# The opening microseconds of a decayed linear-attention layer: smaller idle matmuls that may start sooner, and three small steps moved on VectorE and ScalarE

## The chip, the cores and the metric

One NeuronCore of a Trainium2 chip runs the whole kernel. The metric is the device time of one execution in microseconds, from three runs of the same compiled program; their median is the time before. Five engines work side by side, each in its own program order: TensorE (PE in the rows, its weight loads PEld), VectorE (DVE), ScalarE (ACT), GpSimd (POOL) and SyncE (SP), which issues the transfers. They meet only at semaphores.

## The reference

A layer on x of shape 4 x 512 x 256 (batch, tokens, width), 16 heads of 16 columns. Cut to what matters:

```
xn = layernorm(x)
q, k, v = silu(xn @ Wq), silu(xn @ Wk), silu(xn @ Wv)
# per head, chunks of tokens, log_decay ld (one number per head):
#   scores = (q k^T) * exp(ld * max(i - j, 0)) * (i >= j)      inside a chunk
#   o      = scores v + (q S) * exp(ld * (i + 1))              S: state of the chunks before
#   S      = exp(ld * chunk) * S + (k * exp(ld * (chunk - 1 - i)))^T v
o = rmsnorm_per_head(o * sigmoid(xn @ Wg1 @ Wg2)) * norm_w
s = o @ Wo
g = silu(fp8(xn * scale) @ fp8(W2 * scale1) / (scale * scale1))
out = x + s * g
```

## The kernel before, in words

**Stages.** The work is cut into 8 steps: two pairs of sequences, four blocks of 128 tokens each; a step `n` holds one block of both sequences of a pair (256 tokens). Inside a step two chunks of 64 tokens are worked on side by side. Each engine has one program written out by hand, with steps overlapped: while step `n` is scored and read out, step `n+1` is projected and step `n+2` is normalised and transposed. The order on an engine is the order of the code; nothing else schedules it. This case is about the first 15 us, before step 0 reaches its first scores, and about one place near 25 us.

**Precision.** Weights and activations are split into a high part and a rest (`w_hi`, `w_lo`; `xT_hi`, `xT_lo`), and a product is three matmuls: high by high, high by low, low by high. The high part of Wq and Wv is made on VectorE, that of Wk on ScalarE (`high_w(1)`); all three rests on VectorE (`low_w`).

**The opening, engine by engine.**

- GpSimd makes constants; a counter `s_pool` rises by one with most of them. `minus_half`, `minus_one` and `eps_col` (128x2 each) are done at 4, the 128x128 identity `ident` at 6.
- TensorE waits for 6, runs `idle(43, ...)`, 43 fp32 matmuls of the first 32 columns of `ident` on themselves, whose result is never read; then `transpose_x(0)`, which needs both normalised tiles `xn` (one from ScalarE, one from VectorE); then `keep_warm(2, ...)`, again unread; then `project_q(0)`, 12 matmuls, once `xT_hi` and `w_lo` of Wq are there; then 12 for k transposed, once `w_lo` of Wk is there; then 12 for k in natural order, then `scores(0)`. Each fp32 matmul shows as two in the trace, so 43 show as 86.
- VectorE makes statistics, log decays per position, its tile of `xn`, the split of Wq, `lag_logdecay` (128x1024: lag times log decay for all heads), `xT_lo` of step 0, the rest of Wk, statistics of step 1, `decay_mask` (128x1024, from ScalarE's `lag_decay`), the split of Wv, the copies of Wg1 (`wg1_a`, `wg1_b`), then `exponent(0)` and `magic(0)` (fp8 rounding, from `e4_y`), then the four `mask(0, r)`, which turn scores into `probs`.
- ScalarE makes its tile of `xn`, small exponentials, `xT_hi` of step 0, `w_hi` of Wk, `lag_decay = exp(lag_logdecay)`, loads the table of Silu, and then `q_par` (twice), `kT`, `e4_y`, `k_nat`.
- GpSimd, after the factors for step 1, takes `sum_y(0)`, `round_y(0)`, `decay_k(0)`, `decay_q(0)` and so on, starting with the result of `magic(0)`.

`inv_scales` and `descale` (128x2 and 128x1, from the two scalar inputs) are needed by `silu_ffn(1)` on ScalarE near 27 us; VectorE makes them just ahead of `w2_fp8`, the last step of rounding W2, for which GpSimd's `own_state_end(0)` waits too. In the rows, `e4_` is cut to `e_`, `w2_` and `w_f32` to `w_` and `w_f`, `wg1_` to `wg_`.

Of the kernel before, what the change touches and what calls it, by code (L numbers as in the profile page):

```python
# [9 lines left out]
ALU = mybir.AluOpType  # L10
# [7 lines left out]
def layer_kernel(nc, x, log_decay, Wq, Wk, Wv, Wo, Wg1, Wg2, norm_w, W2, scale, scale1, out):  # L18
# [29 lines left out]
    with ExitStack() as ctx:  # L48
        def sb(name, shape, dt=F32):
            return ctx.enter_context(nc.sbuf_tensor(name, shape, dt))  # L50

        def sem(name):
            return ctx.enter_context(nc.semaphore(name))
# [3 lines left out]
        w_f32 = sb("w_f32", [P, 3, KH, D])  # L57
        w_hi = sb("w_hi", [P, 3, KH, D], F32R)
# [28 lines left out]
        scales = sb("scales", [P, 2])  # L87
        inv_scales = sb("inv_scales", [P, 2])
        descale = sb("descale", [P, 1])
        ld_row = sb("ld_row", [P, H])  # L90
        ld_col = sb("ld_col", [P, KH])
        ident = sb("ident", [P, P])
# [11 lines left out]
        pos_col = sb("pos_col", [P, 1])  # L104
        pos_col64 = sb("pos_col64", [P, 1])
        k_logdecay = sb("k_logdecay", [P, H])
# [8 lines left out]
        minus_half = sb("minus_half", [P, 2])  # L115
# [57 lines left out]
        ps_score = [b_s[:, 0:512], b_s[:, 512:1024], b_o[:, 0:512], b_o[:, 512:1024]]  # L173
# [32 lines left out]
        s_w = [sem(f"w{name}_loaded") for name in "qkv"]  # L206
# [5 lines left out]
        s_scale = [sem(f"scale{n}_loaded") for n in range(2)]  # L212
        s_pool = sem("pool_constants")
        s_dvec = sem("dve_constants")
# [5 lines left out]
        s_whi = [sem(f"w{name}_hi_ready") for name in "qkv"]  # L220
# [84 lines left out]
        def need(eng, s, v):  # L305
            if v > 0:
                eng.wait_ge(s, v)
# [10 lines left out]
        def x_tiles(n):  # L318
            first = S * NB * pair(n) + pos(n)
            return slice(first, first + NB + 1, NB)  # L320
# [245 lines left out]
        def _(act):  # L566
# [11 lines left out]
            def high_xT(n):  # L578
                act.wait_ge(s_xTps, n + 1)
                need(act, s_vps, n - 1)  # L580
                a.activation(xT_hi[:, n % 2], ps_xT, ACT.Copy).then_inc(s_xThi, 1)
# [99 lines left out]
            def high_w(n):  # L681
                act.wait_ge(s_w[n], 16)
                a.activation(w_hi[:, n], w_f32[:, n], ACT.Copy).then_inc(s_whi[n], 1)
# [12 lines left out]
            a.activation(chunk_decay[:], ld_col[:], ACT.Exp, scale=float(C)).then_inc(s_actc, 1)  # L696
            a.activation(k_decay[:], k_logdecay[:], ACT.Exp).then_inc(s_actc, 1)
            high_xT(0)
            high_w(1)
            act.wait_ge(s_laglog, 1)  # L700
            a.activation(lag_decay[:], lag_logdecay[:], ACT.Exp).then_inc(s_actc, 1)
            a.activation(table_load[:, 1:2], eps_col[:, 0:1], ACT.Silu)
            act.wait_ge(s_qps, 1)
            act.wait_ge(s_hpar, 2)
# [81 lines left out]
        def _(dve):  # L786
            v = nc.vector
# [15 lines left out]
            def low_xT(n):  # L803
                dve.wait_ge(s_xThi, n + 1)
                need(dve, s_vps, n - 1)
                v.tensor_tensor(xT_lo[:, n % 2], ps_xT, xT_hi[:, n % 2].bitcast(F32), ALU.subtract).then_inc(s_xTlo, 1)  # L806

            def exponent(n):
                dve.wait_ge(s_y4, n + 1)
                v.tensor_scalar(e4_exp[:].bitcast(I32), e4_y[:, n % 2].bitcast(I32), 0x7F800000, None, ALU.bitwise_and).then_inc(s_exp, 1)  # L810

            def magic(n):
                dve.wait_ge(s_exp, n + 1)
                need(dve, s_e4q, n - 1)
                v.tensor_scalar(e4_magic[:, n % 2], e4_exp[:], E4_MIN, E4_MAGIC, ALU.max, ALU.mult).then_inc(s_e4, 1)  # L815
# [8 lines left out]
            def low_g1(n):  # L824
                dve.wait_ge(s_g1hi, n + 1)
                v.tensor_tensor(g1T[32:64], ps_g1T[32:64], g1T[32:64].bitcast(F32), ALU.subtract).then_inc(s_g1lo, 1)
# [166 lines left out]
            def low_w(n):  # L993
                dve.wait_ge(s_whi[n], 1)
                v.tensor_tensor(w_lo[:, n], w_f32[:, n], w_hi[:, n].bitcast(F32), ALU.subtract).then_inc(s_wlo, 1)
# [23 lines left out]
            for half in range(KH):  # L1019
# [1 line left out]
            dve.wait_ge(s_ldown, KH)  # L1021
            v.tensor_reduce(ld_col[:], ld_own[:], AX_X, ALU.add)
            dve.wait_ge(s_pool, 11)
            v.tensor_scalar(k_logdecay[:], ld_row[:], pos_col[:, 0:1], None, ALU.mult).then_inc(s_dvec, 1)
            v.tensor_copy(ld_units[:].rearrange("p (r k q) -> p r k q", r=4, k=2),
                          ld_row[:].rearrange("p (k r q) -> p r k q", k=2, r=4))
            dve.wait_ge(s_shift, 1)
            v.tensor_scalar(xn[:, 0, 1], x_sb[:, x_tiles(0).start + NB, :], rstd[:, 0, 1:2], shift[:, 0, 1:2], ALU.mult, ALU.add).then_inc(s_xnfirst, 1)
            dve.wait_ge(s_w[0], 16)
            v.tensor_copy(w_hi[:, 0], w_f32[:, 0]).then_inc(s_whi[0], 1)  # L1030
            low_w(0)

            dve.wait_ge(s_dvec, 2)
            v.tensor_tensor(lag_logdecay[:], lag_clamped[:].unsqueeze(1).broadcast_to([P, H, C]),
                            ld_units[:].unsqueeze(2).broadcast_to([P, H, C]), ALU.mult).then_inc(s_laglog, 1)
            low_xT(0)
            low_w(1)
            stats(1)
# [13 lines left out]
                              wg1_f32[:].unsqueeze(2).broadcast_to([P, KH, 3, GR])).then_inc(s_g1w, 1)  # L1052
            dve.wait_ge(s_g1w, 1)
            v.tensor_tensor(wg1_a[:, :, 96:96 + GR], wg1_f32[:], wg1_a[:, :, 0:GR].bitcast(F32), ALU.subtract).then_inc(s_g1w, 1)
            exponent(0)
            magic(0)

# [23 lines left out]
            dve.wait_ge(s_w2sum, 1)  # L1081
            v.scalar_tensor_tensor(out=w2_q[:], in0=w2_f32[:], scalar=-1.0, in1=w2_m[:], op0=ALU.mult, op1=ALU.add).then_inc(s_w2q, 1)
            low_g1(1)
            v.reciprocal(inv_scales[:], scales[:]).then_inc(s_dvec, 1)
            dve.wait_ge(s_dvec, 3)
            v.tensor_scalar(descale[:], inv_scales[:, 0:1], inv_scales[:, 1:2], None, ALU.mult).then_inc(s_dvec, 1)
            dve.wait_ge(s_w2q, 5)
            v.scalar_tensor_tensor(out=w2_fp8[:], in0=w2_over[:], scalar=0.0, in1=w2_q[:], op0=ALU.mult, op1=ALU.add).then_inc(s_w2q, 1)
            put_nan(1)
# [35 lines left out]
            n = STEPS - 1  # L1125
# [20 lines left out]
        def _(pe):  # L1146
            t = nc.tensor

            def transpose_x(n):
                pe.wait_ge(s_xn, n + 1)  # L1150
                if n == 0:
                    pe.wait_ge(s_xnfirst, 1)
                if n == 1:
                    pe.wait_ge(s_y4, 1)
                need(pe, s_on, n - 2)
                if n == 2:
                    pe.wait_ge(s_y4, 2)
                for s in range(S):
                    for kk in range(KH):
                        mm = t.transpose(ps_xT[:, kk, s * P:s * P + P], xn[:, n % 2, s, kk * P:kk * P + P], ident[:])  # L1160
                mm.then_inc(s_xTps, 1)
# [265 lines left out]
            def idle(count, dst):  # L1427

                for _ in range(count):
                    t.matmul(dst[0:32, 0:32], ident[:, 0:32], ident[:, 0:32], start=True, stop=True)  # L1430

            def keep_warm(count, dst):
                for _ in range(count):
                    t.matmul(dst[:, 0:P], ident[:], ident[:], start=True, stop=True)

            pe.wait_ge(s_pool, 6)
            idle(43, ps_score[1])
            transpose_x(0)
            keep_warm(2, ps_score[1])
            pe.wait_ge(s_wlo, 1)  # L1440
# [3 lines left out]
            for part in (w_hi, w_lo):  # L1444
                for half in range(KH):
                    for kk in range(KH):
                        t.matmul(ps_kT[:, half], part[:, 1, kk, half * P:half * P + P], xT_hi[:, 0, kk],
                                 start=(part is w_hi and half == 0 and kk == 0), stop=False, skip_group_check=True)
            for half in range(KH):
                for kk in range(KH):  # L1450
                    mm = t.matmul(ps_kT[:, half], w_hi[:, 1, kk, half * P:half * P + P], xT_lo[:, 0, kk],
                                  start=False, stop=(kk == KH - 1), skip_group_check=True)
# [68 lines left out]
            n = STEPS - 1  # L1521
# [48 lines left out]
```

## Time and profile before

| | us |
|---|---|
| median of 3 runs | 124.86 |
| lowest, highest | 124.48, 125.65 |
| the profiled execution, its whole time | 124.32 |
| its span, first to last instruction | 122.6 |

Busy time in that span: TensorE 114.2 us, VectorE 97.6, GpSimd 89.9, ScalarE 85.0. The profiled execution is 0.54 us below the median of the three, and 1.72 us of its time lie outside the span. A busy share is a mean over the whole span; the change touches the first 15 us, so what counts there is which engine has no idle time in that stretch and which wait ends last.

### The profile page before, as it was taken

The page shows a single profiled execution, that of the slowest core. Times are in us where ns is not written, and L with a number is a line of the kernel's source. Part 1 is how long each engine was busy: PE and PEld are TensorE (multiplying, and loading weights), DVE is VectorE, ACT ScalarE, POOL GpSimd, SP SyncE. Part 2 cuts the span into 40 slices and gives each one's busy share as a digit, 9 for nine tenths or more (in the row PEclk, how much of TensorE's full clock was granted, in tenths as well). Part 3 has the DMA queues.
Part 4 walks back from the last instruction along what each step waited for, and adds up shares of the span by engine and source line. Part 5 has one row for each costly group of instructions (what it writes and reads, how often), then busy time and mean ns, then how long its engine had stood idle before and what let it go on. Part 6 is the DMA issues. An engine that isn't in the chain of part 4 may idle for free.

```text
span 122.6 us, 6549 instructions
## 1 busy us (share of the span) xinstructions
PE 114.2 (93%) x2756; PEld 100.6 (82%) x2756; DVE 97.6 (80%) x264; ACT 85.0 (69%) x164; POOL 89.9 (73%) x126
## 2 busy tenths in 40 slices
PE   3989989998999999999999999999999999899890
PEld 3989879876998899879988898879988997787670
DVE  1899899999998698949994989679975985388572
ACT  7679989889996758766886667685776377932200
POOL 6615499979999899688969696969882996544140
PEclk9999999999999999999999999999999999999999
DMA  2669910002000220024001500042003405000214
GB/s 86 201 176 324 327 38 3 0 5 51 3 5 0 50 46 0 5 56 126 0 3 31 145 5 5 5 92 87 0 5 68 114 0 135 1 5 5 88 34 142
DMA packets 11085, 7.59 MB, mean 62 GB/s; under 512 B 4848, under 2 KB 11056, under 8 KB 11056
## 3 DMA queue, kind: packets, MB, share of 16 engines
q1 hardware_dynamic: 11056, 7.17, 21.1%
q8 instruction: 22, 0.36, 1.3%
q14 instruction: 7, 0.06, 0.2%
HBM read 3.50 MB, written 2.10 MB: 46 GB/s over the span
## 4 chain that ended last, share of the span: by engine, by line
POOL 33%; issue 27%; PE 16%; DVE 15%; ACT 6%; POOLq 0%; DVEq 0%
POOL qd L440 5%; POOL e_sum L430 5%; POOL y L468 5%; POOL kd L446 4%; PE b_s L1430 4%; DVE probs L831 3%; POOL own_mid L450 3%; POOL probs L473 2%; POOL rstd L417 2%; PE b_s L1423 2%; PE b_o L1423 2%; PE b_s L1272 1%; POOL own_end L450 1%; PE b_kv L1342 1%; DVE og L864 1%
## 5 line engine op out<-in xcount | busy, mean ns | idle before, releaser
L1187 PE MATMUL b_kv<-w_hi,xT_hi 128*128 128x256 f32 x64 | 16.6, 283 | 0.0
L1188 PE MATMUL b_kv<-w_lo,xT_hi 128*128 128x256 f32 x64 | 16.4, 280 | 0.0
L430 POOL TENSOR_TENSOR e_sum<-e_y,e_magic 128x512 f32<-128x512 f32 x8 | 10.3, 1286 | 7.4 <-DVE e_magic L815 7.2
L864 DVE SCALAR_TENSOR_TENSOR og<-gate_tanh,b_o 128x512 f32<-128x512 f32 x7 | 4.8, 687 | 11.0 <-PE b_o L1342 11.0
L1190 PE MATMUL b_kv<-w_hi,xT_lo 128*128 128x256 f32 x64 | 12.7, 280 | 0.0
L1342 PE MATMUL b_o<-probs,v_par 64*32 64x64 f32 x896 | 12.4, 223 | 0.0
L1187 PEld LDWEIGHTS b_kv<-w_hi,xT_hi 128*128 128x128 f32 x64 | 12.1, 189 | 0.2 <-issue 0.2
L1188 PEld LDWEIGHTS b_kv<-w_lo,xT_hi 128*128 128x128 f32 x64 | 12.1, 190 | 0.0
L468 POOL TENSOR_TENSOR y<-sg,x_sb 128x512 f32<-128x512 f32 x7 | 9.0, 1288 | 3.9 <-DVE sg L991 3.9
L479 POOL TENSOR_TENSOR on_lo<-on,on_hi 128x512 fp32r<-128x512 f32 x6 | 7.7, 1278 | 5.1 <-ACT on_hi L679 5.1
L435 POOL TENSOR_TENSOR e_q<-e_sum,e_magic 128x512 bf16<-128x512 f32 x8 | 10.8, 1348 | 0.5
L831 DVE TENSOR_TENSOR probs<-b_o,decay_mask 128x512 f32<-128x512 f32 x16 | 10.3, 685 | 1.0 <-PE b_o L1272 0.9
L1342 PEld LDWEIGHTS b_o<-probs,v_par 64*32 64x32 f32 x896 | 9.0, 105 | 2.3 <-issue 1.2
L440 POOL TENSOR_TENSOR qd<-q_silu,q_decay 128x512 f32<-128x512 f32 x8 | 10.4, 1305 | 0.0
L1272 PE MATMUL b_s<-q_par,kT 32*64 32x128 f32 x256 | 9.3, 276 | 1.1 <-DVE og L864 0.7
L596 ACT ACTIVATE q_par<-b_q,head_parity 128x512 f32<-128x512 f32 x16 | 10.1, 683 | 0.0
L473 POOL TENSOR_TENSOR probs<-scores_copy,decay_mask 128x512 f32<-128x512 f32 x7 | 9.1, 1300 | 0.9 <-ACT scores_copy L645 0.9
L1190 PEld LDWEIGHTS b_kv<-w_hi,xT_lo 128*128 128x128 f32 x64 | 9.7, 188 | 0.0
L1272 PEld LDWEIGHTS b_s<-q_par,kT 32*64 32x64 f32 x256 | 7.6, 130 | 2.5 <-issue 2.2
L1272 PE MATMUL b_o<-q_par,kT 32*64 32x128 f32 x256 | 9.6, 278 | 0.0
L586 ACT ACTIVATE e_y<-b_x,scales 128x512 f32<-128x512 f32 x8 | 5.5, 688 | 5.3 <-DVE xT_lo L806 5.3
L591 ACT ACTIVATE q_silu<-b_q 128x512 f32<-128x512 f32 x8 | 4.8, 599 | 6.3 <-PE b_q L1179 6.3
(218 smaller groups left out, 378.7 us busy)
## 6 DMA issues: line engine op xcount, KB each, us to landing
out_dram<-y SPq DMA_DIRECT2D x7, 256.0 KB, 2.4
x_sb<-in_L_attn_x_dram SPq DMA_DIRECT2D x4, 384.0 KB, 6.1
own_cross<-own_end SPq DMA_DIRECT2D x12, 64.0 KB, 2.2
qd_cross<-qd SPq DMA_DIRECT2D x12, 64.0 KB, 2.2
x_sb<-in_L_attn_x_dram SPq DMA_DIRECT2D x2, 128.0 KB, 2.1
w_f<-in_L_attn_Wq_dram SPq DMA_DIRECT2D x1, 256.0 KB, 3.6
w_f<-in_L_attn_Wk_dram SPq DMA_DIRECT2D x1, 256.0 KB, 3.8
x_sb<-in_L_attn_x_dram SPq DMA_DIRECT2D x1, 256.0 KB, 4.0
```

The source lines that it names most:

```text
L430: g.tensor_tensor(e4_sum[:], e4_y[:, n % 2], e4_magic[:, n % 2], ALU.add).then_inc(s_e4sum, 1)
L435: g.tensor_tensor(e4_q[:], e4_sum[:], e4_magic[:, n % 2], ALU.subtract).then_inc(s_e4q, 1)
L440: g.tensor_tensor(qd[:, n % 2].rearrange("p k (s t) -> p k s t", s=S), q_silu[:].rearrange("p k (s t) -> p k s t", s=S), q_decay[:].unsque ...
L468: g.tensor_tensor(y[:, n % 2], sg[:, n % 2].rearrange("p (s d) -> p s d", s=S), x_sb[:, x_tiles(n), :], ALU.add).then_inc(s_y, 1)
L473: g.tensor_tensor(probs[:, 1], scores_copy[:].rearrange("p (s z) -> p s z", s=S), decay_mask[:, 1].unsqueeze(1).broadcast_to([P, S, 4 * C] ...
L596: a.activation(q_par[:, n % 2, par], ps_q, ACT.Silu, scale=head_parity[:, par:par + 1]).then_inc(s_qpar, 1)
L831: v.tensor_tensor(probs[:, r], ps_score[r].rearrange("p (s z) -> p s z", s=S), decay_mask[:, r].unsqueeze(1).broadcast_to([P, S, 4 * C]), ...
L1187: t.matmul(dst[:, s], xT_hi[:, u, kk, tok], w_hi[:, w, kk], start=(s == 0 and kk == 0), stop=False, skip_group_check=True)
L1188: t.matmul(dst[:, s], xT_hi[:, u, kk, tok], w_lo[:, w, kk], start=False, stop=False, skip_group_check=True)
L1190: mm = t.matmul(dst[:, s], xT_lo[:, u, kk, tok], w_hi[:, w, kk], start=False, stop=(kk == KH - 1), skip_group_check=True)
L1272: mm = t.matmul(ps_score[r][c * C:c * C + C, cols], kT[rows, u, half, tok], q_par[rows, u, :, half, tok], start=True, stop=True, skip_grou ...
L1342: mm = t.matmul(dst[32 * r:32 * r + 32, c, z:z + C], v_par[rows, u, blk:blk + 2 * E], probs[rows, r, s, i:i + C], start=(half == 0 and s = ...
```

## The change

Three edits. (1) The idle matmuls take the 128x2 tile `minus_half` as both operands instead of 128x32 of `ident`, and wait for `s_pool` 4 instead of 6; there are still 43 of them. The wait for 6 stays, now behind them. (2) On VectorE `ld_units` goes ahead of `k_logdecay`, and `lag_logdecay` ahead of the split of Wq; on ScalarE `lag_decay` goes ahead of `high_w(1)`. (3) On VectorE the reciprocals and `descale` go from behind `low_g1(1)` to ahead of `exponent(0)`, with a wait for the two loads of the scales.

```
@@ ScalarE
             high_xT(0)
-            high_w(1)
             act.wait_ge(s_laglog, 1)
             a.activation(lag_decay[:], lag_logdecay[:], ACT.Exp).then_inc(s_actc, 1)
+            high_w(1)
@@ VectorE
-            v.tensor_scalar(k_logdecay[:], ld_row[:], pos_col[:, 0:1], None, ALU.mult).then_inc(s_dvec, 1)
             v.tensor_copy(ld_units[:].rearrange("p (r k q) -> p r k q", r=4, k=2),
                           ld_row[:].rearrange("p (k r q) -> p r k q", k=2, r=4))
+            v.tensor_scalar(k_logdecay[:], ld_row[:], pos_col[:, 0:1], None, ALU.mult).then_inc(s_dvec, 1)
             dve.wait_ge(s_shift, 1)
...
+            dve.wait_ge(s_dvec, 2)
+            v.tensor_tensor(lag_logdecay[:], lag_clamped[:].unsqueeze(1).broadcast_to([P, H, C]),
+                            ld_units[:].unsqueeze(2).broadcast_to([P, H, C]), ALU.mult).then_inc(s_laglog, 1)
             dve.wait_ge(s_w[0], 16)
             v.tensor_copy(w_hi[:, 0], w_f32[:, 0]).then_inc(s_whi[0], 1)
             low_w(0)
-            dve.wait_ge(s_dvec, 2)
-            v.tensor_tensor(lag_logdecay[:], ...
             low_xT(0)
...
+            for n in range(2):
+                dve.wait_ge(s_scale[n], 16)
+            v.reciprocal(inv_scales[:], scales[:]).then_inc(s_dvec, 1)
+            dve.wait_ge(s_dvec, 3)
+            v.tensor_scalar(descale[:], inv_scales[:, 0:1], inv_scales[:, 1:2], None, ALU.mult).then_inc(s_dvec, 1)
             exponent(0)
             magic(0)
...
             low_g1(1)
-            v.reciprocal(inv_scales[:], scales[:]).then_inc(s_dvec, 1)
-            dve.wait_ge(s_dvec, 3)
-            v.tensor_scalar(descale[:], inv_scales[:, 0:1], inv_scales[:, 1:2], None, ALU.mult).then_inc(s_dvec, 1)
@@ TensorE
-                    t.matmul(dst[0:32, 0:32], ident[:, 0:32], ident[:, 0:32], start=True, stop=True)
+                    t.matmul(dst[0:2, 0:2], minus_half[:], minus_half[:], start=True, stop=True)
...
+            pe.wait_ge(s_pool, 4)
+            idle(43, ps_score[1])
             pe.wait_ge(s_pool, 6)
-            idle(43, ps_score[1])
             transpose_x(0)
```

What stands in a row on VectorE at the opening (`ld_row` is the row of log decays, `w_f` the loaded weights, Wq first and Wk at the second `w_lo`), and behind the copies of Wg1:

```order
-L1024 TENSOR_SCALAR k_logdecay<-ld_row,pos_col 128x16 [waits pool_constants]
-L1025 COPY ld_units<-ld_row 128x16
+L1024 COPY ld_units<-ld_row 128x16 [waits pool_constants]
+L1026 TENSOR_SCALAR k_logdecay<-ld_row,pos_col 128x16
 L1028 TENSOR_SCALAR xn<-x_sb,rstd,shift 128x256 [waits rstd_shift_ready]
-L1030 CAST w_hi<-w_f 128x512 [waits wq_loaded]
+L1031 TENSOR_TENSOR lag_logdecay<-lag_clamped,ld_units 128x1024 [waits dve_constants]
+L1034 CAST w_hi<-w_f 128x512 [waits wq_loaded]
 L995 TENSOR_TENSOR w_lo<-w_f,w_hi 128x512 [waits wq_hi_ready]
-L1034 TENSOR_TENSOR lag_logdecay<-lag_clamped,ld_units 128x1024 [waits dve_constants]
 L806 TENSOR_TENSOR xT_lo<-b_x,xT_hi 128x512 [waits xT_hi_ready]
```

The 128x1024 product has moved ahead of both steps of Wq's split; behind `xT_lo` nothing has moved until this piece, still on VectorE:

```order
 L1051 CAST wg_b<-wg_f 128x2x3x16
 L1054 TENSOR_TENSOR wg_a<-wg_f,wg_a 128x2x16 [waits wg1_stack_ready]
+L1057 RECIPROCAL inv_scales<-scales 128x2 [waits scale1_loaded,scale0_loaded]
+L1059 TENSOR_SCALAR descale<-inv_scales 128x1 [waits dve_constants]
 L810 TENSOR_SCALAR e_exp<-e_y 128x512 [waits e4_y_ready]
 L815 TENSOR_SCALAR e_magic<-e_exp 128x512 [waits e4_exp_ready]
```

Two steps now stand ahead of `exponent(0)`. On ScalarE, between the small exponentials and the load of Silu's table:

```order
 L697 ACTIVATE k_decay<-k_logdecay 128x16
 L581 ACTIVATE xT_hi<-b_x 128x512
+L700 ACTIVATE lag_decay<-lag_logdecay 128x1024
 L683 ACTIVATE w_hi<-w_f 128x512
-L701 ACTIVATE lag_decay<-lag_logdecay 128x1024
 L702 ACT_TABLE_LOAD
 L702 ACTIVATE table_load<-eps_col 128x1
```

The exponential of the lags and the high part of Wk have changed places; all around them is as it was.

## Rows read from the trace of the kernel before

**Rows 1.** The chain that ended last, opening: start us, us, what

```profile
2.12 4.79 PE b_s L1430 x86
...
7.66 0.60 ACT xT_hi L581
...
8.67 1.05 ACT lag_decay L701
...
9.74 1.28 ACT L702
...
12.88 0.58 ACT e_y L586
```

**Rows 2.** Busy time by engine (PE, PEld, DVE, ACT, POOL), granted clock, in two stretches

```profile
5.00:8.30 3.30, 3.07 (x44) 2.81 (x42) 3.12 (x10) 2.03 (x7) 0.52 (x7) 1.00 0.82 252
8.30:13.00 4.70, 4.54 (x44) 4.37 (x46) 4.67 (x12) 4.67 (x8) 2.84 (x6) 1.00 0.87 263
```

**Rows 3.** VectorE in order of time, opening: start us, us, what

```profile
5.61 0.41 DVE L1028 TENSOR_SCALAR xn<-x_sb,rstd,shift 128x256 f32<-128x256 f32 x1
5.94 0.42 DVE L1030 CAST w_hi<-w_f 128x512 fp32r<-128x512 f32 x1
6.39 0.69 DVE L995 TENSOR_TENSOR w_lo<-w_f,w_hi 128x512 fp32r<-128x512 f32 x1
7.00 1.22 DVE L1034 TENSOR_TENSOR lag_logdecay<-lag_clamped,ld_units 128x1024 f32<-128x1024 f32 x1
8.29 0.69 DVE L806 TENSOR_TENSOR xT_lo<-b_x,xT_hi 128x512 fp32r<-128x512 f32 x1
8.89 0.68 DVE L995 TENSOR_TENSOR w_lo<-w_f,w_hi 128x512 fp32r<-128x512 f32 x1
...
12.83 0.18 DVE L1054 TENSOR_TENSOR wg_a<-wg_f,wg_a 128x32 fp32r<-128x32 f32 x1
13.49 0.43 DVE L810 TENSOR_SCALAR e_exp<-e_y 128x512 int32<-128x512 int32 x1 [0.48 <-ACT e_y L586]
...
14.30 1.28 DVE L831 TENSOR_TENSOR probs<-b_o,decay_mask 128x512 f32<-128x512 f32 x2
```

**Rows 4.** GpSimd in order of time: a constant, and the start of rounding

```profile
1.39 0.09 POOL L487 MEMSET eps_col<- 128x2 f32 x1
...
14.46 1.30 POOL L430 TENSOR_TENSOR e_sum<-e_y,e_magic 128x512 f32<-128x512 f32 x1 [1.50 <-DVE e_magic L815]
```

**Rows 5.** TensorE in order of time, opening

```profile
6.84 0.78 PE L1160 MATMUL b_x<-ident,xn 128*128 128x128 f32 x4
7.46 0.61 PE L1434 MATMUL b_s<-ident 128*128 128x128 f32 x4
8.40 0.71 PE L1174 MATMUL b_q<-xT_hi,w_hi 128*128 128x256 f32 x4 [0.33 <-ACT xT_hi L581]
...
9.89 0.63 PE L1447 MATMUL b_kv<-xT_hi,w_hi 128*128 128x256 f32 x4
...
13.86 0.28 PE L1272 MATMUL b_o<-q_par,kT 32*64 32x128 f32 x2
...
15.54 0.60 PE L1160 MATMUL b_x<-ident,xn 128*128 128x128 f32 x4
```

**Rows 6.** ScalarE in order of time, opening

```profile
5.41 0.60 ACT L691 ACTIVATE xn<-x_sb,shift,rstd 128x256 f32<-128x256 f32 x1 [1.17 <-POOL shift L419]
...
6.59 0.20 ACT L697 ACTIVATE k_decay<-k_logdecay 128x16 f32<-128x16 f32 x1
...
8.15 0.62 ACT L683 ACTIVATE w_hi<-w_f 128x512 fp32r<-128x512 f32 x1
```

**Rows 7.** VectorE in order of time, near 25 us

```profile
24.62 0.17 DVE L1084 RECIPROCAL inv_scales<-scales 128x2 f32<-128x2 f32 x1
...
24.95 0.88 DVE L1088 SCALAR_TENSOR_TENSOR w_fp<-w_over,w_q 128x512 bf16<-128x512 bf16 x1
```

**Rows 8.** GpSimd in order of time, near 25 us

```profile
25.91 0.61 POOL L450 TENSOR_TENSOR own_end<-state_end,own_quad 128x256 f32<-128x256 f32 x1 [0.63 <-DVE w_fp L1088]
```

**Rows 9.** The chain that ended last, near 25 us

```profile
25.31 0.61 ACT b_s L603
```

More of the change, by code:

```diff
@@ L1031, in _ @@
             low_w(0)
-            dve.wait_ge(s_dvec, 2)
-            v.tensor_tensor(lag_logdecay[:], lag_clamped[:].unsqueeze(1).broadcast_to([P, H, C]),
-                            ld_units[:].unsqueeze(2).broadcast_to([P, H, C]), ALU.mult).then_inc(s_laglog, 1)
             low_xT(0)
```

## The prediction

> **What bounds the kernel now.** I read three views, in this order. First the chain that ended last, because it names what a reader would cut: in the opening it runs through the idle matmuls (86 rows, 4.79 us), `xT_hi` on ScalarE, `lag_decay`, the table load and `e_y` [rows 1]. Read alone, it promises that shorter idle matmuls and an earlier `lag_decay` pass straight on to the end. The second view is the busy time by stretch [rows 2], which shows what the chain can't: a second engine with no slack. VectorE is busy 3.12 of 3.30 us in the first stretch and 4.67 of 4.70 in the second, while ScalarE is busy 2.03 of 3.30 in the first. The third is VectorE in order of time [rows 3]: from `xn` at 5.61 to the last copy of Wg1, which ends at 12.83 + 0.18 = 13.01, its steps stand shoulder to shoulder; its only real pause is the 0.48 us ahead of `e_exp` at 13.49, where it waits for ScalarE's `e_y`. GpSimd starts its long row of 1.3 us products at 14.46, on the result that follows this `e_exp` [rows 4]. So the time at which `e_exp` starts stands for the end of the opening: before 13.49, VectorE needs 13.01 and ScalarE 13.46. A change that frees ScalarE alone can win at most 0.48 us there, less what it adds to VectorE.
>
> **Idle matmuls.** Now they start when `ident` is done, at 2.12, and end at 6.91. The new ones need only `eps_col`, done at 1.39 + 0.09 = 1.48 [rows 4], so they start 0.6 us sooner. What one with two columns takes no row shows. Upper bound: what one of 32 columns takes, 4.79 / 86 = 56 ns; they then end at 1.5 + 4.8 = 6.3. Lower: four with 128 columns take 0.61 us, 153 ns each [rows 5]; a straight line through 32 and 128 columns falls by 1 ns a column and gives 25 ns for two, 2.2 us in all, an end near 3.7. I take no value between, since for the next step both ends are near the same: the transposes need both tiles of `xn`, which end at 5.41 + 0.60 = 6.01 on ScalarE [rows 6] and at 5.61 + 0.41 = 6.02 on VectorE [rows 3]. They start at 6.05 (6.3 at the upper bound) in place of 6.84, a gain of 0.8 (0.55). The wait for `s_pool` 6 behind the idle matmuls costs nothing: `ident` is long done.
>
> **Lags ahead of weights, ScalarE.** `xT_hi` started 7.66 - 6.84 = 0.82 behind the first transpose [rows 1, 5]; now at 6.87, and ScalarE is free from 6.59 + 0.20 = 6.79 [rows 6]. `lag_decay` follows 0.49 later, as `w_hi` did (8.15 - 7.66), at 7.36; its input is there, since `lag_logdecay` now runs from 5.94 and takes 1.22 [rows 3], to 7.16. `high_w(1)` starts 1.07 behind it (9.74 - 8.67), at 8.43, and ends at 9.05. The table load follows 0.52 behind its start, at 8.95 in place of 9.74. So ScalarE's lead is 0.79 us, and `e_y` ends at 12.88 + 0.58 - 0.79 = 12.67.
>
> **Lags ahead of weights, VectorE.** The order changes, not the sum: 5.94 + 1.22 (lags) + 0.45 (`w_hi`) + 0.61 (`w_lo`) = 8.22, where `lag_logdecay` ended before, too (7.00 + 1.22). `xT_lo` waited for `xT_hi` until 8.29 and no longer does: 0.07 gained. `w_lo` of Wq moves from 7.08 to about 8.30, and `project_q(0)` waits for that now and not for `xT_hi`: it starts at 8.3, before 8.40 [rows 5]. So TensorE gets back 0.1 of the 0.8. Then comes the price. The rest of Wk waits for its high part, which ScalarE now has at 9.05 and had at 8.15 + 0.62 = 8.77: that step starts at 9.08, before 8.89. VectorE stands there for 0.2 us, with the statistics of step 1, `decay_mask` and the split of Wv queued behind it: +0.19 on all of them, and the copy of Wg1 ends at 13.20. If the transposes start at 6.3, 0.25 later, it is +0.44. TensorE's matmuls for k transposed start with that `w_lo`, at 9.8, before 9.89. GpSimd clears `wg1_a` and `wg1_b` when `lag_logdecay` is done, sooner now, in a stretch where it has 0.52 us of work in 3.30 [rows 2]: nothing.
>
> **Reciprocals sooner.** Two steps, from 24.62 to 24.95 [rows 7]: 0.33 us, now ahead of `e_exp`. Their new wait for the scales costs nothing, since ScalarE uses the first for `e_y` itself, and the second is issued with the loads of the first 8 us; if it came late, `e_exp` and the masks would stand behind it. Sum for `e_exp`: 13.20 + 0.33 = 13.53, against 13.49 before. **The pause of 0.48 us is used up**, 0.19 by the later Wk and 0.33 by the reciprocals. At the bounds: 13.01 - 0.07 + 0.33 = 13.27 (-0.22) with no stall on Wk, and 13.01 + 0.44 + 0.33 = 13.78 (+0.29) with the late transposes. The masks then start at 14.34, before 14.30; the scores ended at 13.86 + 0.28 = 14.14 [rows 5], and come a little sooner.
>
> Near 25 us 0.33 is given back, but `w_fp` also waits for ScalarE's `w_over`, so I count 0.13 of it. GpSimd's `own_end` waited for `w_fp` until 25.91 [rows 8] and moves up by that. The chain doesn't pass there: it goes through ScalarE's `b_s` at 25.31 [rows 9], which neither gives way to `w_fp` nor follows it. 0 at the end; bounds 0 and -0.13.
>
> **Sum.** +0.04 at the opening, 0 near 25 us; bounds -0.35 and +0.29. Every later step follows by the same waits, so this is also the sum for the end. I take the middle of the bounds, -0.03: the profiled execution, 124.32 (span 122.6), becomes 124.3; the median of the runs, 0.54 above it, 124.86 becomes **124.8**.
>
> **Rivals.** (a) *ScalarE's lead arrives.* If VectorE's row is elastic (steps that run faster when GpSimd is quiet, or a stall on Wk that doesn't come), the chain of waits is right and up to 0.79 us goes to the end: 124.86 - 0.8 = 124.1. For it: [rows 1]. Against it: [rows 2, 3], and 0.33 us of new work at the very place.
>
> (b) *The small matmul isn't shorter.* If one with two columns takes 56 ns as now, the change doesn't shorten the idle stretch, only shifts it by 0.6: `e_exp` at 13.78, 124.86 + 0.3 = 125.1. For it: the rows of 128 and 32 columns say nothing of a floor. Against it: the straight line.
>
> (c) *TensorE's clock, the slower side.* The rows grant 1.00, the 2.4 GHz level, in both stretches [rows 2], with TensorE at work without a pause from 2.1 to 8.1. The four first transposes took 0.78 us, the four at 15.54 took 0.60 [rows 5], so I don't take for certain that the first ones ran at the full pace. After the change TensorE works on two columns at a time and may then stand from about 3.7 to 6.05, 2.3 us that were filled before. If the level is 1.2 GHz when the projections come, their 36 matmuls, which take 9.89 - 8.40 = 1.49 us per 12, take up to twice that. With half of the 36 at the low level: 2.2 us more; the scores have 14.30 - 14.14 = 0.16 of slack and start 0.3 sooner, so 1.7 reaches the masks: 126.6. It passes 1% (1.25 us) from about 14 matmuls at the low level on; all 36 give 129. The page "TensorE: Matmul & The Clock Gate" of the Trainium skill speaks for this rival (section "What's actually happening"): "the default state is throttled, and activity releases the throttle." No row here shows a fall or a rise, so I can't say from the trace whether such small matmuls hold the clock; that they are the kernel's only work in those microseconds is what makes this the widest risk.
>
> **Chances.** Forecast 0.48, (a) 0.17, (b) 0.15, (c) 0.20. A measurement of this kernel tells about 1% from no change; the three runs before spread by 0.9%. Forecast, (b) and most of (a) lie within 1%. Faster by over 1%: 0.06 from (a), where other luck adds to it, and 0.02 from the forecast, 0.08. Slower: 0.17 from (c), 0.02 from (b), 0.19. Within: 0.73. Range: from (a) less 0.5 for the spread of the runs, 123.6, up to 126.2, which takes in (b) and the cheap part of (c).
>
> **What would show it.** In the profile after: idle matmuls from 1.5, transposes at 6.05 to 6.3; `lag_decay` near 7.4; the second `w_lo` waiting for ScalarE until 9.1; the table load near 9.0; `e_exp` between 13.3 and 13.8 with no wait for `e_y` ahead of it; `e_sum` at 14.5. (a) is right if `e_sum` starts before 14.1, (b) if the idle matmuls still take 4.8, (c) if the projections' starts lie further apart than 0.12 us or the granted clock is below 1.00. Wrong altogether would be a gain over 1.2 us: then a loop later than 15 us would have fallen into another rhythm, which no term here covers.

## Result, and the profile after

| | before | after |
|---|---|---|
| median of the runs taken together, us | 124.72 (6 runs, 124.44 to 125.65) | 126.30 (6 runs, 125.87 to 126.90) |
| ratio, 95% interval | | 1.0126, 1.0081 to 1.0171 |
| profiled execution, us | 124.32 | 126.31 |
| its span, us | 122.6 | 124.5 |

The change makes the kernel slower by 1.6 us at the medians. The time was forecast as 124.8, with 123.6 to 126.2 as the range; the outcome is the rival (c), TensorE's clock. Here and in the experiments a ratio leaves out the runs more than 1.5% above the fastest of the same kernel, while the medians are of all runs.

TensorE in order of time in the changed kernel, opening (the columns are start us, us, what):

```profile
1.54 2.29 PE L1432 MATMUL b_s<-minus_half 128*2 128x2 f32 x86 [1.54 <-POOL eps_col L487]
6.31 1.08 PE L1162 MATMUL b_x<-ident,xn 128*128 128x128 f32 x4 [2.49 <-DVE xn L1028]
7.19 1.06 PE L1436 MATMUL b_s<-ident 128*128 128x128 f32 x4
8.42 1.22 PE L1176 MATMUL b_q<-xT_hi,w_hi 128*128 128x256 f32 x4 [0.17 <-DVE w_lo L995]
9.44 1.05 PE L1176 MATMUL b_q<-xT_hi,w_lo 128*128 128x256 f32 x4
10.29 1.05 PE L1181 MATMUL b_q<-xT_lo,w_hi 128*128 128x256 f32 x4
11.15 1.05 PE L1450 MATMUL b_kv<-xT_hi,w_hi 128*128 128x256 f32 x4
12.00 0.90 PE L1450 MATMUL b_kv<-xT_hi,w_lo 128*128 128x256 f32 x4
12.74 0.63 PE L1454 MATMUL b_kv<-xT_lo,w_hi 128*128 128x256 f32 x4
```

The idle matmuls end at 3.8 and TensorE stands for 2.49 us. Then read the starts, not the busy time: four 256-column matmuls take 11.15 - 10.29 = 0.86 us from start to the next group's start, 0.215 each, which is 256 columns at 1.2 GHz; before, [rows 5], the first row of such matmuls and the row of the k projection are 12 matmuls and 1.49 us apart, 0.12 each, 256 columns at 2.4 GHz. From 12.00 to 12.74 four take 0.74, so the pace changes inside them, near 12.6: three at 0.215, one at 0.12. By then 19 of the 36 matmuls of the projections have been started at the lower level. The first transposes, too, take 0.88 from start to start of the next group, where those of [rows 5] took 7.46 - 6.84 = 0.62 and those of a later step less still.

The granted clock of the windows of the changed kernel (the 1.00 ahead of the last two numbers) says nothing of it:

```profile
8.00:10.00 2.00, 1.83 (x9) 1.58 (x8) 1.44 (x3) 1.98 (x4) 0.14 (x1) 1.00 0.57 111
12.00:14.00 2.00, 2.00 (x16) 2.00 (x16) 1.92 (x8) 1.25 (x4) 1.53 (x4) 1.00 1.03 327
```

Both stretches read 1.00, the 2.4 GHz level, and TensorE is busy in both; only the counts tell, 9 matmuls in the first and 16 in the second. The trace explains the column. It keeps a list of stretches with a recorded clock, and the first of them, at 1.00, begins at 12.58 us, where the starts change; for the time ahead of it there is no record, and a window without one reads 1.00. In the kernel before, the first record begins at 7.14. So 1.00 in the opening means "nothing recorded", and the starts give the level: 1.2 GHz.

VectorE in the changed kernel, the rows that answer to [rows 3]:

```profile
6.08 1.22 DVE L1031 TENSOR_TENSOR lag_logdecay<-lag_clamped,ld_units 128x1024 f32<-128x1024 f32 x1
7.22 0.42 DVE L1034 CAST w_hi<-w_f 128x512 fp32r<-128x512 f32 x1
7.67 0.69 DVE L995 TENSOR_TENSOR w_lo<-w_f,w_hi 128x512 fp32r<-128x512 f32 x1
8.28 0.68 DVE L806 TENSOR_TENSOR xT_lo<-b_x,xT_hi 128x512 fp32r<-128x512 f32 x1
9.53 0.69 DVE L995 TENSOR_TENSOR w_lo<-w_f,w_hi 128x512 fp32r<-128x512 f32 x1 [0.56 <-ACT w_hi L683]
...
14.62 0.43 DVE L810 TENSOR_SCALAR e_exp<-e_y 128x512 int32<-128x512 int32 x1 [0.63 <-ACT e_y L586]
...
16.03 1.29 DVE L831 TENSOR_TENSOR probs<-b_o,decay_mask 128x512 f32<-128x512 f32 x2 [0.52 <-PE b_o L1274]
```

The rest of Wk waits for ScalarE, as forecast, but 0.56 us instead of 0.2, since the transposes ahead of `xT_hi` start at 6.31 and run at the lower pace. `e_exp` now waits 0.63 for `e_y`, and the masks, which had no wait before, wait 0.52 for the scores: they start at 16.03, before 14.30. ScalarE shows the same from its side:

```profile
7.43 0.60 ACT L581 ACTIVATE xT_hi<-b_x 128x512 fp32r<-128x512 f32 x1 [0.61 <-PE b_x L1162]
7.93 1.05 ACT L700 ACTIVATE lag_decay<-lag_logdecay 128x1024 f32<-128x1024 f32 x1
...
11.39 1.27 ACT L596 ACTIVATE q_par<-b_q,head_parity 128x512 f32<-128x512 f32 x2 [0.38 <-PE b_q L1181]
13.41 0.60 ACT L707 ACTIVATE kT<-b_kv 128x512 f32<-128x512 f32 x1 [0.75 <-PE b_kv L1454]
```

`lag_decay` starts 0.74 us sooner than in [rows 1], and the lead is lost twice, at both waits for TensorE. Of the 1.9 us by which the span grew, 1.73 are there when the masks start. The next step is later still: its `xT_lo` starts at 19.46, before 17.32, which is 2.14; experiment 1 shows where the rest comes from.

### The profile page after: what moved, and what is told of

The parts are those of the page before. It is cut to its first block, busy times and chain, and to the rows that moved or that the text cites. A ratio compares the mean times of both kernels' runs of the same rounds, so it can differ in the third digit from the quotient of the medians.

```text
span 124.5 us, 6550 instructions
## 1 busy us (share of the span) xinstructions
PE 114.8 (92%) x2756; PEld 100.9 (81%) x2756; DVE 98.3 (79%) x264; ACT 85.6 (69%) x164; POOL 89.9 (72%) x126
## 4 chain that ended last, share of the span: by engine, by line
POOL 32%; issue 27%; DVE 18%; PE 15%; DMA 3%; ACT 3%; SPq 1%; POOLq 0%; DVEq 0%
POOL qd L440 5%; POOL e_sum L430 5%; POOL y L468 5%; POOL kd L446 4%; DVE probs L831 3%; POOL own_mid L450 3%; DMA ld_row<-in_L_attn_log_decay_dram 3%; POOL rstd L417 2%; POOL probs L473 2%; PE b_s L1274 2%; PE b_q L1176 2%; PE b_s L1425 2%; POOL own_end L450 1%; PE b_kv L1450 1%; PE b_kv L1344 1%
## 5 line engine op out<-in xcount | busy, mean ns | idle before, releaser
L440 POOL TENSOR_TENSOR qd<-q_silu,q_decay 128x512 f32<-128x512 f32 x8 | 10.5, 1318 | 0.0
```

The source lines that it names most:

```text
L440: g.tensor_tensor(qd[:, n % 2].rearrange("p k (s t) -> p k s t", s=S), q_silu[:].rearrange("p k (s t) -> p k s t", s=S), q_decay[:].unsque ...
```

## The experiments

Each kernel ran beside the kernel before on one chip. Twelve experiments; "masks" is the start of the first `probs` on VectorE in the profiled execution, "pace" the time at which TensorE's starts change from the lower to the higher pace. It is where the trace's first clock record begins, and in each case the starts change there; only experiment 5 has no record, and its time is from the starts alone.

| kernel | median, us (runs) | before | ratio, 95% interval | pace | masks |
|---|---|---|---|---|---|
| before | | | | 7.1 | 14.30 |
| changed | 126.30 (6) | 124.72 | 1.0126, 1.0081 to 1.0171 | 12.6 | 16.03 |
| 1, small idle alone | 126.63 (4) | 125.03 | 1.0150, 1.0057 to 1.0243 | 10.5 | 14.84 |
| 2, moves alone | 125.54 (10) | 125.03 | 1.0072, 1.0025 to 1.0119 | 5.7 | 14.34 |
| 3, changed, small idle longer | 126.99 (4) | 125.03 | 1.0191, 1.0111 to 1.0272 | 12.3 | 15.76 |
| 4, changed, wide idle early | 125.00 (10) | 125.03 | 1.0021, 0.9983 to 1.0059 | 6.4 | 14.25 |
| 5, wide idle early alone | 124.68 (12) | 125.06 | 0.9969, 0.9936 to 1.0003 | 5.8 to 6.1 | 13.71 |
| 6, lags alone | 125.50 (12) | 125.06 | 1.0025, 0.9996 to 1.0054 | 7.5 | 15.03 |
| 7, reciprocals alone | 125.13 (12) | 125.06 | 1.0005, 0.9976 to 1.0034 | 6.2 | 13.93 |
| 8, no idle | 129.00 (4) | 125.06 | 1.0298, 1.0252 to 1.0344 | 10.4 | 14.75 |
| 9, changed, again | 125.99 (10) | 125.07 | 1.0030, 0.9985 to 1.0075 | 10.0 | 14.69 |
| 10, small idle alone, again | 125.97 (10) | 125.07 | 1.0047, 1.0007 to 1.0087 | 9.1 | 14.16 |
| 11, wide idle early, lags | 124.78 (12) | 125.07 | 0.9982, 0.9951 to 1.0013 | 5.4 | 14.06 |
| 12, wide idle early alone, again | 124.81 (12) | 125.07 | 1.0011, 0.9984 to 1.0038 | 6.2 | 13.88 |

The theory was that the small idle matmuls leave TensorE at the lower clock (C). Its rival was that the moved steps and the stall on Wk do the harm (M).

**1. Small idle alone.** The first edit on the kernel before, without the moves.

```
-                    t.matmul(dst[0:32, 0:32], ident[:, 0:32], ident[:, 0:32], start=True, stop=True)
+                    t.matmul(dst[0:2, 0:2], minus_half[:], minus_half[:], start=True, stop=True)
...
-            pe.wait_ge(s_pool, 6)
+            pe.wait_ge(s_pool, 4)
             idle(43, ps_score[1])
+            pe.wait_ge(s_pool, 6)
```

> Only the idle matmuls are changed (43 on the 128x2 tile, start at 1.5 us), the moves on VectorE and ScalarE are not made. Theory C (TensorE runs the projections at the slower pace because its small idle matmuls end at 3.8 us and leave a pause): the first projections stand 0.21 us apart as in the changed kernel, the masks start 1.5 to 2 us later than 14.30, time 126.0 to 126.6. Theory M (the moved steps and the stall on Wk cost it): time within 0.4 us of before, 124.7, projections 0.12 us apart.

126.63, and the lower pace is there. TensorE in this kernel:

```profile
6.20 1.08 PE L1160 MATMUL b_x<-ident,xn 128*128 128x128 f32 x4 [2.37 <-ACT xn L691]
...
9.05 1.05 PE L1174 MATMUL b_q<-xT_hi,w_lo 128*128 128x256 f32 x4
9.91 0.90 PE L1179 MATMUL b_q<-xT_lo,w_hi 128*128 128x256 f32 x4
10.64 0.63 PE L1448 MATMUL b_kv<-xT_hi,w_hi 128*128 128x256 f32 x4
```

The first edit by itself makes the whole loss at the medians. In the profiled execution, whose span is 2.2 us longer than before, only 0.54 us of it stands at the masks (14.84), less than the 1.5 to 2 expected. Another 0.46 joins before the next step's `xT_lo` starts (18.32, before 17.32). VectorE and GpSimd in this kernel, then in the kernel before:

```profile
17.24 1.16 DVE L1063 TENSOR_SCALAR w_m<-w_y 128x512 int32<-128x512 int32 x1
17.05 1.05 POOL L446 TENSOR_TENSOR kd<-k_nat,k_decay 128x512 f32<-128x512 f32 x1
```

```profile
16.69 0.71 DVE L1063 TENSOR_SCALAR w_m<-w_y 128x512 int32<-128x512 int32 x1
17.07 1.24 POOL L446 TENSOR_TENSOR kd<-k_nat,k_decay 128x512 f32<-128x512 f32 x1
```

VectorE's `w_m` takes 1.11 to 1.16 us in the four traces where it starts behind GpSimd's `kd` (changed, 1, 3, 8), and 0.42 to 0.72 in the ten where it starts ahead of it. GpSimd's row starts behind `e_exp`, and `w_m` stands behind the masks, so masks that wait long for the scores put `w_m` behind `kd`. No run moves this step by itself, so that `kd` slows it is a reading of the fourteen traces and not shown. The last microsecond comes from a later step, with a pause inside its scores, told below.

**2. Moves alone.** The changed kernel with the idle matmuls of before.

> The idle matmuls are those of before (32 columns of ident, from 2.1 us), the moves on VectorE and ScalarE and the earlier reciprocals are made. Theory C: 124.3 to 125.1, near the time before, with the second w_lo and e_exp some tenths later than before. Theory M: 125.8 to 126.4, as the changed kernel.

125.54, 0.7% above before, between the two forecasts: not the harm of (M), and not nothing. Masks at 14.34, 0.04 later than in the trace before, though the pace changed 1.5 us earlier in this execution (its 86 idle matmuls take 4.35 us and not 4.79, and so end at 6.47). The rest of this execution's loss stands later: GpSimd's `e_sum` is 0.05 behind the kernel before at 21.80, and 0.58 at 56.25. Experiments 6, 7 and 11 take the opening apart.

**3. The pause closed by small matmuls.** The changed kernel with more of them.

```
-            idle(43, ps_score[1])
+            idle(92, ps_score[1])
```

> The changed kernel with 92 small idle matmuls in place of 43: at 25 ns for each of 184 rows they run from 1.5 to about 6.1 us, so the pause ahead of the transposes is closed by two-column work. If the pause alone made the pace fall (theory C, pause), projections 0.12 us apart and 124.0 to 125.0. If two-column matmuls don't count as work for the clock however many there are (theory C, size), projections 0.21 us apart at first and 125.9 to 126.6.

```profile
1.54 4.74 PE L1432 MATMUL b_s<-minus_half 128*2 128x2 f32 x184 [1.54 <-POOL eps_col L487]
6.21 1.12 PE L1162 MATMUL b_x<-ident,xn 128*128 128x128 f32 x4
7.11 1.06 PE L1436 MATMUL b_s<-ident 128*128 128x128 f32 x4
```

No pause is left, the transposes show no wait, and the pace still changes only at 12.3; 126.99, 0.4 above the forecast. So the pause isn't the cause: TensorE's row reads as fully busy from 1.54 on, and its clock isn't raised. What is left is the matmul itself, its size or its numbers (every element of `minus_half` is the same); the two aren't told apart here. The page "TensorE: Matmul & The Clock Gate" of the Trainium skill (section "What's actually happening") says that activity releases the throttle. Here 4.74 us that the profile counts as busy throughout were followed by a rise no sooner than in the kernel with no idle matmuls at all (12.3, and 10.4 in experiment 8).

**4. Wide idle, early.** The changed kernel with 32 columns again, of a tile that is ready at 1.15 us.

```
-                    t.matmul(dst[0:2, 0:2], minus_half[:], minus_half[:], start=True, stop=True)
+                    t.matmul(dst[0:32, 0:32], pos_row[:, 0, 0:32], pos_row[:, 0, 0:32], start=True, stop=True)
...
-            pe.wait_ge(s_pool, 4)
+            pe.wait_ge(s_pool, 1)
```

> The changed kernel with idle matmuls of 32 columns again, 43 of them, on the first 32 columns of pos_row, which is ready at about 1.15 us: they run from 1.2 to about 6.0. Theory C in both forms: projections 0.12 us apart, perhaps from an earlier time than before; transposes at 6.1; 123.9 to 124.8. Theory M: 125.8 to 126.4.

125.00, 0.2 above the forecast. With every moved step in place the time is that of before, which refutes (M) for the main loss: 1 to 2 us depend on the operands of 43 matmuls whose results nobody reads. `pos_row` differs from `minus_half` in its numbers as well as in its width.

**5. Wide idle early, alone.** The same on the kernel before, no moves.

> The kernel before with its 43 idle matmuls of 32 columns on pos_row instead of ident, from 1.2 us to about 6.0, no moves. Transposes at 6.2 in place of 6.84 and the clock up by then; VectorE is full from 5 to 13 us, so the opening gains only what its pause gives back. Theory V (VectorE sets the end of the opening): masks between 13.9 and 14.25, time 124.4 to 124.9. Rival (a) of the prediction (the lead arrives): masks near 13.6, time 124.0 to 124.3.

```profile
1.20 4.80 PE L1430 MATMUL b_s<-pos_row 128*32 128x32 f32 x86 [1.20 <-POOL pos_row L482]
6.11 0.63 PE L1160 MATMUL b_x<-ident,xn 128*128 128x128 f32 x4
6.58 0.61 PE L1434 MATMUL b_s<-ident 128*128 128x128 f32 x4
7.52 0.71 PE L1174 MATMUL b_q<-xT_hi,w_hi 128*128 128x256 f32 x4 [0.33 <-ACT xT_hi L581]
```

```profile
12.90 0.43 DVE L810 TENSOR_SCALAR e_exp<-e_y 128x512 int32<-128x512 int32 x1 [0.23 <-ACT e_y L586]
...
13.71 1.28 DVE L831 TENSOR_TENSOR probs<-b_o,decay_mask 128x512 f32<-128x512 f32 x2
```

Transposes at 6.11 at the high pace, `e_exp` at 12.90 (13.49 before), masks at 13.71: 0.59 us sooner at the opening, more than theory V allowed, and 0.38 us at the medians. It adds up from three parts: VectorE runs 0.18 earlier from its first steps in this execution (`w_lo` of Wq at 6.21, 6.39 in [rows 3]), which is luck; `xT_lo` no longer waits for `xT_hi` (7.96, another 0.15); and the pause of 0.48 shrinks to 0.23. That these come from the earlier idle matmuls isn't shown by this trace alone: experiment 7 has the idle matmuls of before and masks at 13.93, in an execution whose pace rose at 6.2 and not at 7.1.

**6. Lags alone** (second edit on the kernel before).

> Only lag_logdecay and lag_decay are moved ahead of the weights' parts; idle matmuls and reciprocals as before. Theory V: the second w_lo waits for ScalarE by some tenths, but e_exp has 0.48 us of pause to take it up: masks at 14.2 to 14.4, time within 0.3 us of before. If the moves did the harm seen in the run with the moves alone (0.5 us): about 125.5.

125.50, masks at 15.03. This execution got the higher pace late, at 7.5, and its transposes are slow; then the chain that the moves have laid over ScalarE does its harm:

```profile
8.48 0.69 DVE L806 TENSOR_TENSOR xT_lo<-b_x,xT_hi 128x512 fp32r<-128x512 f32 x1 [0.46 <-ACT xT_hi L581]
9.95 0.69 DVE L995 TENSOR_TENSOR w_lo<-w_f,w_hi 128x512 fp32r<-128x512 f32 x1 [0.78 <-ACT w_hi L683]
```

VectorE stands for 1.24 us in a stretch where it stood 0.07 before. The expectation of 14.2 to 14.4 was wrong by 0.6: with the transposes not sooner, the later Wk costs all of `lag_decay`, as `high_w(1)` now waits for it. `e_exp` starts at 13.99, only 0.50 later than before, since the old pause takes up the rest; the masks are later by 0.73 because the scores are: TensorE's matmuls for k wait 0.50 for that `w_lo`, and the masks wait 0.15 for the scores.

**7. Reciprocals alone** (third edit). 

> Only the two steps for descale are moved to ahead of e_exp(0). They fit into the pause of 0.48 us (0.33 of it): e_exp at 13.5, masks at 14.3, no change at 25 us or up to 0.13 less; time within 0.3 us of before. If they are the harm in the run with the moves alone: about 125.5.

125.13, 1.0005 (0.9976 to 1.0034), `e_exp` at 13.12 and no wait ahead of it, masks at 13.93 with the pace up at 6.2. The two steps fit into the pause, as expected: beside experiment 12, whose VectorE row is otherwise within 0.02 us of this one up to the copies of Wg1, `e_exp` is 0.04 later. Both times are 0.4 sooner than forecast, which goes with the earlier rise of the clock; no gain near 25 us is to be seen in the time.

**8. No idle.**

```
-            idle(43, ps_score[1])
```

> The kernel before with no idle matmuls at all. If two-column matmuls count for nothing with the clock, this is as slow as the run with the small idle matmuls alone: low pace until 10 to 12.5 us, 126.2 to 127.0. If they count for something, it is slower than that by half a microsecond or more: 127.2 or above.

129.00, which would be the second forecast, but its opening is that of experiment 1: pace up at 10.4, masks at 14.75 (14.84 there). The rest is no matter of the clock, whose record reads 1.00 from 10.4 to 126.4. The last `e_sum` starts at 97.29, 0.23 behind experiment 1, and the span ends 2.7 behind it. The chain that ended last, near the end of this kernel:

```profile
114.17 1.10 PE b_kv L1342 x72
115.27 1.61 issue
116.88 0.46 PE b_kv L1342 x31
```

TensorE stops for 1.61 us between two matmuls of one loop, waiting for nothing that the profile shows, and VectorE waits 2.55 us for it. So the comparison with experiment 1 is spoilt in its totals and holds only in the openings, where one execution each shows no worth of the two-column matmuls at all. As the rise moves from run to run (experiments 9 and 10), that is weak evidence.

**9 and 10. The same kernels again.**

> The changed kernel once more, for the place at which TensorE's pace changes. Seen so far: about 12.2 us in its trace, 10.4 in the trace with the small idle matmuls alone. If the place is fixed by the program (the later start of the projections): again 12.2, masks at 16.0. If it varies from run to run: anywhere from 9 to 13, masks from 14.6 to 16.5. Time 125.8 to 127.0 in either case.

> The small idle matmuls alone once more. Place of the change of pace fixed by the program: 10.4 again, masks at 14.8. Varying: another place than 10.4, and the masks move with it. Time 125.3 to 127.1.

The place of the change of pace isn't fixed by the program: 10.0 now for the changed kernel against 12.6, 9.1 for the small idle alone against 10.5. TensorE in experiment 9:

```profile
9.20 0.99 PE L1176 MATMUL b_q<-xT_hi,w_lo 128*128 128x256 f32 x4
10.03 0.63 PE L1181 MATMUL b_q<-xT_lo,w_hi 128*128 128x256 f32 x4
```

The masks move with it, to 14.69 and 14.16, and so do the times: these executions took 124.54 and 124.45, the first ones 126.31 and 126.55. The ten runs of the changed kernel go from 124.54 to 128.53, where 35 of the kernel before go from 123.47 to 125.90. The means are 126.19 and 125.07, the standard deviations 1.16 and 0.53, so here the change costs 1.1 us on average and doubles the scatter. The ratio in the table, 1.0030, is smaller than that of these means, 1.009. The six runs of the first comparison cost 1.6 us and scatter no more than those of before (0.40 and 0.46). All 16 have a mean of 126.28.

**11. Wide idle early with the lags' move**, reciprocals where they were.

> Wide idle matmuls on pos_row from 1.2 us, with the lags moved ahead of the weights' parts on both engines, the reciprocals where they were before. It splits the 0.54 us by which the masks are later with all moves (14.25) than with none (13.71). If the reciprocals' 0.33 us is most of it: masks at 13.9, second w_lo waiting about 0.3. If the lags' move is most of it: masks at 14.1 to 14.3. Time 124.6 to 125.2.

Masks at 14.06, between 13.71 to 13.88 without moves and 14.25 with all: the lags' move costs 0.2 to 0.35 and the reciprocals another 0.2. Neither of the two outcomes named was right. But the halves don't stand on one engine. `e_exp` starts at 13.02, no later than without the moves (13.08 in experiment 12), so the stall on Wk is taken up by the old pause; the masks wait 0.15 for the scores, since `project_q(0)` waited 0.90 for the `w_lo` of Wq that the lags' product now delays. With the reciprocals too (experiment 4) `e_exp` starts at 13.46, and the masks wait for nothing but VectorE. In time the kernel can't be told from experiments 5 and 12 (124.78).

**12. Wide idle early alone, again.**

> Wide idle matmuls on pos_row from 1.2 us and nothing else, once more, since 0.3% is as much as five rounds tell. Masks at 13.6 to 13.9, time 0.2 to 0.5 us under before, if the first reading was not chance; the same as before within 0.1% if it was.

Ratio 1.0011 (0.9984 to 1.0038), median 124.81 against 125.07. Masks at 13.88, with VectorE's first steps at the times of [rows 3] (`w_lo` of Wq at 6.39): 0.42 sooner than before with VectorE as early as there. The pace rose at 6.2, though, 0.9 us sooner than in the one trace of the kernel before, and experiment 7 reached 13.93 with the idle matmuls of before and such an earlier rise; so how much of the 0.42 belongs to the earlier idle matmuls stays open. The 24 runs of experiments 5 and 12 have a mean of 124.84. A gain of 0.2 to 0.4 us is suggested by the medians and not shown by the ratios.

## Why the prediction was wrong

**The step that failed is TensorE's clock, which the sum put at nothing.** The sum has no term for it, on the strength of the granted clock of 1.00 in [rows 2]; it was left to rival (c) with a chance of 0.20, against 0.48 for the forecast. The runs showed the lower pace from the first transposes to 12.6 us, and 1.73 us at the masks. The mechanism, the place and the price of (c) were as written: "With half of the 36 at the low level" the masks would be 1.7 us late and the time 126.6; the trace had 19 of the 36 there, the masks 1.73 late, and 126.3. (That the whole time was met owes something to luck: 0.4 us more joined at `w_m`, which the prediction doesn't have, and some of it was regained by the end.) The sentence "No row here shows a fall or a rise" was the mistake. The rows did show a rise: the four first transposes took 0.62 us from their start to that of the next group [rows 5]; at the low pace four take 0.88 (the changed kernel), at the high one 0.47 (experiment 5), so the rise falls inside the group, and the trace's first clock record begins there, at 7.14. And the idle matmuls stood 54 ns apart from the first to the last, where those behind the rise in experiments 2, 7 and 11 stand 31 to 32 apart. These rows say that the 1.00 of [rows 2] isn't a reading of the clock ahead of 7.14, and that TensorE begins at the low level. With that, (c) asks only whether the clock rises as soon behind two columns as behind thirty-two.

**Idle matmuls.** Start at 1.54 and end at 3.8, as the lower bound said (25 ns each, by the starts). That this was met is luck: the straight line joined a row at the low pace (56 ns for 32 columns) with one at the high pace (153 for 128); with 54 and 220 ns, both at the low pace and by the starts, it would have given under 5 ns for two. Transposes at 6.31, where 6.05 to 6.3 was forecast. Of the gain of 0.8 us on them 0.53 was there, and was taken back in part by their own pace.

**Lags, ScalarE.** The order of starts was right; each came later by what the transposes lost: `lag_decay` 7.93 (7.36), table load 9.51 (8.95).

**Lags, VectorE.** The stall on Wk exists and was the right place to look: 0.56 us in the changed kernel (0.71 when run again, 0.70 in experiment 3), 0.43 in experiment 2, 0.27 in 4, 0.25 in 11, 0.78 in 6, for a forecast of 0.2. It was mis-sized in that it hangs on the start and the pace of the transposes. Where these were early and quick (4 and 11), 0.2 held nearly; where they were quick and started at 6.39 (experiment 2), the prediction's own 0.44 for late transposes did. With the lags' move and no reciprocals (6 and 11) it isn't this stall but TensorE's scores that set the masks.

**Reciprocals.** As forecast. The sum for `e_exp`, 13.53, was met at 13.55 in experiment 2 and 13.46 in experiment 4, and the masks, 14.34, at 14.34 and 14.25. So the working for VectorE stands for the kernel in which the clock rises in time. What it hid is that its zero is a sum: earlier transposes, by the idle matmuls or by an earlier rise, bring the masks to 13.7 to 13.9 (experiments 5, 7 and 12), and the moves take about 0.4 us of that back (experiments 2 and 4).

**Rival (a)** has something for it: where the transposes came sooner and no step was added or moved, the masks were 0.4 to 0.6 us sooner than in the trace of before (experiments 5 and 12), through the shrinking pause and the end of a wait, and the medians 0.3 to 0.4. **Rival (b)** is refuted: one of two columns takes 25 ns and not 56.

**Sum and range.** The later rhythm was taken as fixed ("Every later step follows by the same waits"). It isn't: beside `w_m`, a pause of TensorE inside a series of matmuls falls into some executions. GpSimd's `e_sum` has steps of 13.0 to 13.3 us in experiment 1 from 43.67 to 83.03, but then one of 14.03, where the kernel before has 13.13:

```profile
83.03 1.27 POOL L430 TENSOR_TENSOR e_sum<-e_y,e_magic 128x512 f32<-128x512 f32 x1 [1.16 <-DVE e_magic L815]
...
97.06 1.28 POOL L430 TENSOR_TENSOR e_sum<-e_y,e_magic 128x512 f32<-128x512 f32 x1 [2.20 <-DVE e_magic L815]
```

and TensorE in the same place stands between two matmuls of `scores`:

```profile
83.08 0.27 PE L1272 MATMUL b_s<-q_par,kT 32*64 32x128 f32 x1
83.95 0.32 PE L1272 MATMUL b_s<-q_par,kT 32*64 32x128 f32 x1 [0.60 <-issue]
```

The same place shows such a pause in other kernels too, so it isn't the first edit's. From start to start it is 0.87 us in experiments 1 and 12, 0.73 in 11 and 0.5 to 0.6 in 4, 5 and 7; their last steps are 14.03, 14.01, 13.89 and 13.65 to 13.75, where traces without a pause there have 13.13 to 13.20 (before, changed, 2 and 9). The pause passes on to the step nearly whole. What stays open: why this pause comes (a packet of the queue for instructions moves near the one of experiment 8, which is a hint and no proof); whether two-column matmuls are worth exactly nothing; whether their width or their equal numbers matter; and how wide an idle matmul has to be, which wasn't tried.

## What to carry to other kernels

Before making work smaller or cheaper that is there only to hold TensorE's clock, check by the starts of the next real matmuls that the pace survives; the busy share and the clock of a window didn't show it here, the latter because it reads 1.00 where nothing was recorded. Read a suspected clock from starts against columns (256 columns in 0.215 us or in 0.12), in several executions, because the moment of the rise moves from run to run by microseconds; one trace of the kernel before is no firm baseline either. And an opening in which two engines are both nearly full gives back little of a step freed on one alone; test each part by itself, since a gain and a loss of half a microsecond can sum to a quiet zero.

## What the runs showed of the hardware that was not expected

- In a stretch for which the window's clock reads 1.00, TensorE's matmuls of 256 columns stood 0.215 us apart (8.4 to 12.6 us of the changed kernel), the 1.2 GHz pace. The clock is recorded only from the first rise on (12.58 us there), and in thirteen of the fourteen traces that record begins where the starts change; the fourteenth (experiment 5) has none and still reads 1.00.
- 184 two-column matmuls in an unbroken row of 4.74 us were followed by a rise at 12.3 us only, and the six traces with two-column idle matmuls or none had it between 9.1 and 12.6; with 86 of 32 columns in 4.35 to 4.80 us it came between 5.4 and 7.5 us in each of the eight traces that had them.
- The moment of the rise varies between executions of one kernel: 12.6 and 10.0, 10.5 and 9.1.
- An fp32 matmul of two columns costs 25 ns for each of its two rows at the lower clock, where one of 32 costs 54, and 31 to 32 at the higher one.
- VectorE's `w_m` (128x512) took 1.11 to 1.16 us in the four traces where it started behind GpSimd's `kd`, and 0.42 to 0.72 in the ten where it started ahead.
- TensorE can pause inside a series of matmuls, with nothing awaited that the profile shows: 0.5 to 0.87 us from start to start near 82 us in six of the fourteen traces, 1.61 us at 115 us in the kernel with 86 fewer instructions.
